# Score bank filled by ScalarE, VectorE's order in the shifted layers, and the experts' bias and gathers

## What is computed

```python
for i in range(6):
    x = attn_layer(shift_tokens(x), Wqkv[i], q_scale[i], k_scale[i], Wo[i]) + x
    x = ffn_layer(shift_tokens(x), ln_g[i], ln_b[i], W1[i], b1[i], W2[i], b2[i]) + x
# in attn_layer: q, k normed, scaled and rotated; then per window
sim = einsum('bhwie,bhwje->bhwij', q, k2) * 8
sim = where(mask, -finfo.max, sim)      # band: own window and the one before
out = softmax(sim) @ v2
# in ffn_layer: (a * gelu(gate)) @ W2 + b2, a and gate from layernorm(x) @ W1 + b1
```

```python
xin = xf[routes]                                  # 8 x 512 rows gathered
h = gelu(einsum('ekd,edf->ekf', xin, W1) + b1)
out = (einsum('ekf,efd->ekd', h, W2) + b2) * route_vals
final = zeros.at[routes].add(out)                 # rows added back
```

## Time and profile before

| | us |
|---|---|
| median of 3 runs (4852.14 to 4854.57) | 4854.38 |
| the profiled execution | 4843.04 |
| its span, first to last instruction | 4841.2 |
| shifted layers, about | 340 to 3900 |
| experts' gathers, products and additions | 4703 to 4841 |

### The profile page before, as it was taken

The page is one execution under the profiler, slowest core; times in us unless marked ns, Lnnn a source line. Parts: engine busy times, 40 slices in busy tenths (PEclk is TensorE's granted clock), DMA queues, the critical chain, the costliest instruction groups (busy, mean ns, idle before and its releaser), DMA issues. The chain is left out here.

```text
span 4841.2 us, 113325 instructions
## 1 busy us (share of the span) xinstructions
PE 4259.6 (88%) x40622; PEld 2404.1 (50%) x40622; DVE 3564.2 (74%) x8488; ACT 2826.2 (58%) x5112; POOL 2217.0 (46%) x1393
## 2 busy tenths in 40 slices
PE   8969999999999999999999999999999964746646
PEld 5645555554555555545555555555555532535534
DVE  6878888887888888878888888788888847456430
ACT  3436666666666666666666666666666635645301
POOL 0006555555555555555555555555555510030015
PEclk9989999999999999999999999999999975868558
DMA  1012222322223222232222322223222210000202
GB/s 40 1 59 65 59 58 55 78 59 56 58 53 77 64 54 59 54 77 62 54 56 60 74 63 54 58 56 74 61 60 54 58 25 1 12 1 6 77 11 30
DMA packets 187686, 245.93 MB, mean 51 GB/s; under 512 B 88661, under 2 KB 129367, under 8 KB 187224
## 3 DMA queue, kind: packets, MB, share of 16 engines
q1 hardware_dynamic: 181912, 239.95, 21.3%
q0 software_dynamic: 5632, 4.33, 0.7%
HBM read 41.13 MB, written 14.30 MB: 11 GB/s over the span
## 5 line engine op out<-in xcount | busy, mean ns | idle before, releaser
L1229 POOL TENSOR_TENSOR f_rot_a<-f_rot_a,f_norm 128x1024 f32<-128x1024 f32 x384 | 731.1, 1904 | 1106.7 <-DVE f_norm L1072 1074.2
L1221 POOL TENSOR_TENSOR f_rot_a<-f_rot_a,f_rot_b 128x1024 f32<-128x1024 f32 x384 | 907.4, 2363 | 353.8 <-issue 298.3
L830 PE MATMUL f_bank<-f_w_vo,f_xs_t 128*64 128x512 f32 x3072 | 828.5, 617 | 9.7 <-ACT f_vo L1297 9.7
L1297 ACT ACTIVATE f_vo<-f_bank 128x512 f32<-128x512 f32 x768 | 457.7, 596 | 579.0 <-PE f_bank L830 572.6
L1288 ACT ACTIVATE f_squares<-f_bank 128x512 f32<-128x512 f32 x768 | 459.1, 598 | 330.2 <-PE f_bank L817 244.5
L1051 DVE TENSOR_TENSOR f_rot_a<-f_bank,f_rot 128x512 f32<-128x512 f32 x768 | 526.8, 686 | 86.3 <-POOL f_rot_a L1221 41.6
L1054 DVE TENSOR_TENSOR f_rot_b<-f_bank,f_rot 128x512 f32<-128x512 f32 x768 | 514.2, 670 | 0.0
L1100 DVE TENSOR_REDUCE f_stat<-f_score 128x8 f32<-128x512 f32 x384 | 262.0, 682 | 280.5 <-ACT f_score L1314 280.5
L1058 DVE TENSOR_REDUCE f_sums<-f_squares 128x16 f32<-128x1024 f32 x384 | 465.1, 1211 | 3.3
L1309 ACT ACTIVATE f_k_t<-f_bank 64x512 f32<-64x512 f32 x768 | 450.4, 586 | 4.8 <-PE f_bank L852 0.3
L817 PE MATMUL f_bank<-f_w_qk,f_xs_t 128*128 128x512 f32 x768 | 431.7, 644 | 7.4 <-ACT f_xs_t L1279 5.9
(11 more groups left out here) (447 smaller groups left out, 7249.8 us busy)
## 6 DMA issues: line engine op xcount, KB each, us to landing
f_vo_off<-f_vo SPq DMA_DIRECT2D x1152, 128.0 KB, 2.3
f_vo_off<-f_vo SPq DMA_DIRECT2D x384, 64.0 KB, 2.0
f_w_qk<-in_Wqk SPq DMA_DIRECT2D x12, 512.0 KB, 5.5
f_vo_dram<-f_vo_pair SPq DMA_DIRECT2D x48, 128.0 KB, 1.8
f_x_shifted<-s_all SPq DMA_DIRECT2D x48, 128.0 KB
f_x_shifted<-s_all SPq DMA_DIRECT2D x48, 127.0 KB
f_w_vo<-f_vo_dram SPq DMA_DIRECT2D x10, 512.0 KB, 4.0
e_w<-in_e_W SPq DMA_DIRECT2D x2, 2048.0 KB
```

Source lines behind the costliest of these rows:

```text
L830: done = nc.tensor.matmul(bank[V][64 * n:64 * n + 64, :], x, w_vo[:, 4 * g:4 * g + 4, n, :], start=True, stop=True)
L1221: nc.gpsimd.tensor_tensor(rot_a[:, slot, :, :], rot_a[:, slot, :, :], rot_b[:, g, :, :], ALU.add).then_inc(rot_summed, 1)
L1229: nc.gpsimd.tensor_tensor(heads, heads, over(norm[:, 16 * g:16 * g + 16], [128, 16, HEAD_DIM]), ALU.mult).then_inc(qk_normed, 1)
L1297: nc.scalar.activation(vo[:, g, 2 * (t % 2) + j, :], flat(V), ACT.Copy).then_inc((va_copied, vb_copied)[j], 1)
```

## The change

1. **Band by ScalarE.** The matmul at L859 goes. One such matmul is done once, before the loop (`s_opened`). In its place ScalarE copies `band` (bf16, SBUF) into bank S by an activation with Copy, `seed(p, t, g)`, after the key copy of the same tile and half; `seed` takes over the wait for `shifted`, and `scores` waits for `seeded`.
2. **VectorE's order.** In step 3, `hide(p-2, 0)`, and in step 1 `store(p-3)`, come before the second part of the key rotation `rotate(p, r, 1, 1, 1)` and not after it. `hide(p-2, 1)` comes before `highest(p, r-1, 1)` and not after the query rotations and `aggregate`. The `total(p, r-1, 1)` that ended step 2 moves into step 3, behind the first key rotation; `invert(1)` follows it there.
3. **ScalarE's order.** In step 3 the `exponential(p, r-2, 1)` comes after `copy_values(r-1, 1, 0)` and `copy_q(r-1, 0)`.
4. **Experts' bias.** b2 is laid out over all 128 partitions by the host (512 KB are loaded in place of 4 KB); the four bias matmuls of each expert go; VectorE adds b2 to the whole bank in one instruction (128 x 512, PSUM to `rows`), waits for it, and then multiplies the four parts in place in SBUF.
5. **Gathers.** `BESIDE` is four: after each expert's additions four gathers follow. The memset of the ones goes.

```diff
@@ shifted_layers, TensorE
             pe.wait_ge(zeroed, 2)
+            nc.tensor.matmul(flat(S), ident_bf[:, :], band[:, 0, :], start=True, stop=True).then_inc(s_opened, 1)
...
             def scores(p, t, g):
                 pe.wait_ge(k_t_made, count(p, 2 * t + g))
-                pe.wait_ge(shifted, count(p, 2 * t + g - 1))
-                nc.tensor.matmul(flat(S), ident_bf[:, :], band[:, t % 2, :], start=True, stop=True)
+                pe.wait_ge(seeded, count(p, 2 * t + g))
@@ shifted_layers, VectorE's body
-                    if on(r - 2):
+                    if r < 3 and on(r - 2):
                         invert(1)
                     if on(r):
                         rotate(p, r, 0, 1, 1)
+                    if r == 3 and on(r - 2):
+                        total(p, r - 2, 1)
+                        invert(1)
...
                         highest(p, r - 1, 0)
-                    if on(r):
-                        rotate(p, r, 1, 1, 1)
                     if r == 1 and has(p, 3):
                         store(p - 3)
                     if r == 3 and has(p, 2):
                         hide(p - 2, 0)
+                    if on(r):
+                        rotate(p, r, 1, 1, 1)
...
                         total(p, r - 1, 0)
                         invert(0)
+                    if r == 3 and has(p, 2):
+                        hide(p - 2, 1)
+                    if on(r - 1):
                         highest(p, r - 1, 1)
...
                         aggregate()
-                    if r == 3 and has(p, 2):
-                        hide(p - 2, 1)
-                    if on(r - 1):
+                    if r != 2 and on(r - 1):
                         total(p, r - 1, 1)
@@ shifted_layers, ScalarE
+            def seed(p, t, g):
+                act.wait_ge(shifted, count(p, 2 * t + g - 1))
+                nc.scalar.activation(flat(S), band[:, t % 2, :], ACT.Copy).then_inc(seeded, 1)
...
-                    if on(r - 2):
+                    if r < 3 and on(r - 2):
                         exponential(p, r - 2, 1)
                     if on(r - 1):
                         copy_values(p, r - 1, 1, 0)
                         copy_q(p, r - 1, 0)
+                    if r == 3 and on(r - 2):
+                        exponential(p, r - 2, 1)
...
                         copy_k(p, r - 1, 0)
+                        seed(p, r - 1, 0)
                         copy_values(p, r - 1, 1, 1)
...
                         exponential(p, r - 1, 0)
                         copy_k(p, r - 1, 1)
+                        seed(p, r - 1, 1)
@@ apply_experts
-    BESIDE = 2
+    BESIDE = PARTS
...
-            nc.gpsimd.memset(ones[:, :], 1.0).then_inc(ones_set, 1)
...
-                        nc.tensor.matmul(o_bank[e % 2][:, 128 * t:128 * t + 128], h[:, e % 2, c, 128 * t:128 * t + 128], w2[:, e, c, :],
-                                         start=c == 0, stop=False)
-                    last = nc.tensor.matmul(o_bank[e % 2][:, 128 * t:128 * t + 128], ones[:, :], b2[:, DIM * e:DIM * e + DIM], start=False, stop=True)
+                        last = nc.tensor.matmul(o_bank[e % 2][:, 128 * t:128 * t + 128], h[:, e % 2, c, 128 * t:128 * t + 128], w2[:, e, c, :],
+                                         start=c == 0, stop=c == CHUNKS - 1)
...
+                nc.vector.tensor_tensor(rows[:, e % 2, :, :], o_bank[e % 2][:, :].rearrange("p (c n) -> p c n", n=DIM),
+                                        b2[:, DIM * e:DIM * e + DIM].unsqueeze(1).broadcast_to([128, PARTS, DIM]), ALU.add).then_inc(bias_added, 1)
+                dve.wait_ge(bias_added, e + 1)
                 for c in range(PARTS):
-                    last = nc.vector.tensor_scalar(rows[:, e % 2, c, :], o_bank[e % 2][:, 128 * c:128 * c + 128], taken[:, e % RING, c, DIM + e:DIM + e + 1], None, ALU.mult)
+                    last = nc.vector.tensor_scalar(rows[:, e % 2, c, :], rows[:, e % 2, c, :], taken[:, e % RING, c, DIM + e:DIM + e + 1], None, ALU.mult)
```

More of the change, by code:

```diff
@@ L569, in shifted_layers @@
         scores_done, shifted, exped, inverted = sem("scores_done"), sem("shifted"), sem("exped"), sem("inverted")
+        s_opened, seeded = sem("s_opened"), sem("seeded")
         prob_made, prob_turned, prob_t_made = sem("prob_made"), sem("prob_turned"), sem("prob_t_made")
@@ L1265, in _ @@
             act.wait_ge(zeroed, 2)
+            act.wait_ge(s_opened, 1)
             act.wait_ge(rot_out, 16)
@@ L1268, in _ @@
                 act.sem_inc(semaphore, AHEAD)
-            for semaphore in (scores_done, q_turned, k_turned, q_done, k_done, va_done, vb_done, prob_turned, mixed):
+            for semaphore in (seeded, scores_done, q_turned, k_turned, q_done, k_done, va_done, vb_done, prob_turned, mixed):
                 act.sem_inc(semaphore, AHEAD)
@@ L2729, in experts @@
         b1 = ctx.enter_context(nc.sbuf_tensor("e_b1", [128, EXPERTS * CHUNKS], F32))
-        b2 = ctx.enter_context(nc.sbuf_tensor("e_b2", [1, EXPERTS * DIM], F32))
+        b2 = ctx.enter_context(nc.sbuf_tensor("e_b2", [128, EXPERTS * DIM], F32))
         slots = ctx.enter_context(nc.sbuf_tensor("e_slots", [128, EXPERTS, CAPACITY // 128], I32))
@@ L3231, in apply_experts @@
         t_bank = ctx.enter_context(nc.psum_tensor("ea_t_bank", [128, 512], F32))
-        ones = sb("ones", [1, 128])
         taken = sb("taken", [128, RING, PARTS, ROW])
@@ L3236, in apply_experts @@
         rows = sb("rows", [128, 2, PARTS, DIM])
-        ones_set = sem("ones_set")
         gathered = [sem(f"gathered{i}") for i in range(RING)]
@@ L3240, in apply_experts @@
             sem("x_turned"), sem("x_t_made"), sem("h_done"), sem("h_made"), sem("o_done"), sem("rows_made"))
-        added = sem("added")
+        added, bias_added = sem("added"), sem("bias_added")
         ctx.callback(clear, nc, used)
@@ L3303, in second_product @@
                     for c in range(CHUNKS):
-                        nc.tensor.matmul(o_bank[e % 2][:, 128 * t:128 * t + 128], h[:, e % 2, c, 128 * t:128 * t + 128], w2[:, e, c, :],
-                                         start=c == 0, stop=False)
-                    last = nc.tensor.matmul(o_bank[e % 2][:, 128 * t:128 * t + 128], ones[:, :], b2[:, DIM * e:DIM * e + DIM], start=False, stop=True)
+                        last = nc.tensor.matmul(o_bank[e % 2][:, 128 * t:128 * t + 128], h[:, e % 2, c, 128 * t:128 * t + 128], w2[:, e, c, :],
+                                         start=c == 0, stop=c == CHUNKS - 1)
                 last.then_inc(o_done, 1)
             pe.wait_ge(w_in, 64)
-            pe.wait_ge(ones_set, 1)
             turn(0)
@@ L3342, in _ @@
         def _(dve):
+            dve.wait_ge(w_in, 64)
             for e in range(EXPERTS):
@@ L3471, in lay_out @@
     d["e_b1"] = c(f["L3_ffn_b1"].reshape(EXPERTS * CHUNKS, 128).T)
-    d["e_b2"] = c(f["L3_ffn_b2"]).reshape(1, EXPERTS * DIM)
+    d["e_b2"] = c(np.broadcast_to(f["L3_ffn_b2"].reshape(1, EXPERTS * DIM), (128, EXPERTS * DIM)))
     d["k_proj"] = c(f["L1_xattn_projection"].T)
```

## The result

The changed kernel takes 4659.59 us in the median of four runs (4656.79 to 4664.66), the kernel before 4853.26 in its four: a ratio of 0.9604, interval 0.9592 to 0.9617. It is 194 us faster; 183 were forecast. The profiled execution took 4656.79 us, where 4660 was forecast for it.

What follows compares the result with a forecast made beforehand. It took the layers as bound by TensorE's stream and its waits, the experts' end by GpSimd's queue. Layers 3.4 us x 48 = 163 plus experts 20 gave 183 us: 4660 profiled, 4671 median; own range 4635 to 4705, outer 4605 to 4755.

Steps and rivals of the forecast that it cites:

- The band: Layers: dropping eight band matmuls per pass saves TensorE 4 x 0.21 + 4 x 0.32 = 2.1 us, bounds 1.7 and 2.5.
- The seed's price: ScalarE's copy of the band into PSUM takes 0.60 us, of which 0.50 is added to its stream.
- Its slacks: Before scores, g = 0: 0.5 us in step 0, 0.05 step 1, 0.9 step 2; g = 1: 0.2 or more.
- The orders: New orders in the layers cut TensorE's waits from 3.5 to 2.2 us per pass, saving 1.3.
- the walk through step 3: Key turn's 1.31 us wait goes; scores wait 0.75 for the seed; second up projection waits 0.55, values 0.64.
- The experts: GpSimd's queue sets the end; the last addition starts at 4811.3, not 4830.8: gain 19.5 us, range 12 to 22.
- the first addition starts near 4729.3: Experts: GpSimd's first addition comes then, not at 4730.79; TensorE is 2.3 us earlier, VectorE's step 0.8 longer.
- More goes: Layers: new step 3 wait and the one for `hide(0)` don't appear; 271 + 20 us gained, 4563; chance 0.12.
- ScalarE takes TensorE's place: Each seed costs 1.0 us in ScalarE's stream, or copies shift waits; 1.4 us per pass less, 4738; chance 0.22.
- slower: Copying into a bank TensorE also uses is much dearer; at 1.7 us a seed 4896 in all; chance 0.07.
- Layers don't move: Waits go elsewhere on VectorE; only the experts give, 8 to 20 us, 4834 to 4846; chance 0.04.
- The rule against it: Experts' SBUF multiplications and GpSimd lock each other out; experts give 8 us, not 20; chance 0.4 within any case.

Runs made afterwards that it cites:

- experiment 6: Changed kernel with hide(0) in step 3 and store in step 1 moved ahead of one more rotation and highest(0): 0.9511 of the kernel before.
- experiment 4: Changed kernel with a second copy of the band, into a spare buffer, ahead of every seed: 0.9820 of the kernel before, 105 us over the change.
- experiment 5: Changed kernel with the layers' gelus replaced by Copy, so no table load before the exponential: 0.9489 of the kernel before.
- both halves: Kernel before with the experts' part alone, bias on VectorE and four gathers behind each expert's additions: 0.9959.
- gathers only: Kernel before with four gathers behind each expert's additions, bias still matmuls on TensorE: 0.9961.
- bias only: Kernel before with the experts' bias on VectorE, still two gathers behind each expert's additions: 0.9975.
- experiments 5 to 8: Changed kernel with gelus as Copy, 0.9489; separately feed-forward earlier, 0.9511, then added in turn: later probability copy, 0.9496, later third gelu, 0.9481, three gathers, 0.9473.
- band only: Kernel before with the band copied by ScalarE, orders and experts as before: 0.9864, 66 us.
- orders only: Kernel before with the new orders of VectorE and ScalarE, band still a matmul, experts as before: 0.9751, 121 us.
- every seed twice: Changed kernel with one more copy of the band, into a spare tile, before each seed: 0.9820 of the kernel before.
- experiment 3: Kernel before with the experts' part alone, 0.9959, its gathers alone, 0.9961, or its bias on VectorE alone, 0.9975.

## Why the prediction was right, point by point

- **What bounds the kernel:** right. The layers are TensorE's stream plus its waits; an edit of VectorE's order alone (experiment 6) took away two waits of 0.99 us a pass and gave 45 us.
- **The band:** right to 0.1 us, 2.18 a pass where 2.1 was taken. Taking 0.21 after a full tile and 0.32 after a narrow one was the right reading of the earlier trace rows. What it is worth alone is less, 1.42, since two waits take a third back.
- **The seed's price:** right. I took 0.60 us, and 0.50 of it in the stream. It lasts 0.583, and from the key copy before it to the next copy ScalarE takes 1.10 us where it took 0.62, so 0.49 in the stream. ScalarE's row for the seed:

```profile
L1321 ACT ACTIVATE f_bank<-f_band x384: 582/583/584, 358.0 to 3721.1; 128x512 f32<-128x512 bf16 x192
```

- **Its slacks:** partly wrong. Step 0 has 0.4 us for g = 0 and 0.06 for g = 1 (experiment 4). The sum behind them does not come out either: the terms that I listed for step 0 leave 0.2 us (2.39 less 2.2), not 0.5, and 0.3 us is likewise missing in steps 1 and 2. At 0.58 us a copy only step 3 pays for it; at 1.1 four places do. The rival of a dear seed would therefore have been dearer than I priced it: 2.07 us a pass for 0.54 more in the stream, not 1.4.
- **The orders:** the walk through step 3 held to 0.1 us at each place of the table. For the scores its own terms give 6.88 - 6.22 = 0.66 us, which is what was measured; I booked 0.75. The step that paid most, query copy ahead of the table load, was predicted at 1.31 us and is 1.30. The new wait at the scores is real, and experiment 5 ties it to the table load.
- **The experts:** the terms were right in the kernel with nothing else changed (19.2 for 19.5). In the change 5.3 us are missing; the step that failed is "the first addition starts near 4729.3", 25.2 us after the first gather; after the change that would be 4557.2, and it was 4562.4. The second product, complete at 4554.9, was in time for it; what is late is TensorE's signal that it is complete, at 4560.45, in the slow stretch.
- **The sum** is right in part by luck. Trace against trace the gain is 186 us: 172 ahead of the first gather, 14 behind it, where 163 and 20 were forecast, so an error of +9 and one of -5. Of the 172, 167 lie between the first and the last fold (47 passes by 3.55) and 5 behind the last, in a stretch of some 890 us that also differs by 4 us between kernels whose layers are the same. Within the 167 there is luck as well: a full pass gives 3.7 and not 3.4 (the walk lacked the two ends of tiles, 0.14, and had the wait at the seed 0.09 too long), but the first nine give 2.9. The 194 us between the medians are some 7 more than the traces show: the profiled execution of the kernel before is 10 us under the median of its runs, that of the change 3. No trace shows where those 7 us lie.
- **The range.** 4605 and 4755 are not halfway to the neighbours, as the prediction says; halfway to 4563 and 4738 is 4617 and 4704. The measured 4660 lies inside either, and in the narrower 4635 to 4705.
- **The rivals.** More goes: no, the two waits appeared as walked. ScalarE takes TensorE's place, and slower: no, at 583 ns. Layers don't move: no. The parts are not independent, however: 66 and 121 us alone, 172 together.
- **The rule against it** came true in a small part and cost nothing. The multiplications from SBUF beside GpSimd's additions:

```profile
L3364 DVE TENSOR_SCALAR ea_rows<-ea_rows,ea_taken x32: 279/284/595, 4561.3 to 4630.0; 128x128 f32<-128x128 f32 x32
...
L3279 POOL DMA_INDIRECT out<-ea_rows,e_slots x32: 1550/1566/1641, 4562.4 to 4644.5; - x32
```

284 ns in the median, less than the 343 ns that they took from PSUM, and additions of 1566 ns where they were 1567. But the 595 in the row is no stray: in each of the last three experts the third multiplication takes 594 or 595 ns and the fourth 465, in the change and, within 2 ns, in both halves alone. From PSUM none took over 352. They are under way in the middle of an addition on GpSimd; one such expert (the four multiplications are merged in the row, 1.06 us for the 0.88 of the first expert):

```profile
4629.28 1.55 POOL L3279 DMA_INDIRECT out<-ea_rows,e_slots  x1 [2.47 <-DMA out<-ea_rows,e_slots]
4629.37 1.06 DVE L3364 TENSOR_SCALAR ea_rows<-ea_rows,ea_taken 128x128 f32<-128x128 f32 x4
```

So VectorE is held up beside GpSimd, by up to 0.3 us a multiplication. The prediction had the size and the price wrong. It hits 6 of 32 multiplications in full, the additions don't grow, and these rows are ready a whole round of additions before GpSimd takes them, so the stage pays nothing. The Trainium skill, SBUF — State Buffer, "Who interferes with whom", describes a lock between the two engines for a whole instruction. The trace agrees in part: the long ones end 1.1 us into an addition of 1.55, and the first and second multiplication of these experts, which run in its first 0.6 us, take 280 to 291 ns. I had given the lock a chance of 0.4. I had taken the layers' median of 706 ns as the nearest row; what lengthens those runs beside the layers' GpSimd work was not tried.

## What stays open

The slow stretch in the experts. It lasts about 5 us some 20 us after the first gather, in the change, in gathers only, in bias only and in all kernels of experiments 5 to 8 (the wait before the first addition is 5.0 to 5.4 us), and it is missing in the kernel before and in band only, orders only, both halves and every seed twice (0.3 to 1.8 us). The last has the very experts' code of the change. So neither bias nor gathers nor data decide. What does is open: the program as a whole, the chip or the single execution, since each kernel was traced once and the chips split just as the stretch does (experiment 3). One more thing goes with it and is not explained. In the 60 us after the first gather the eight traces with the stretch hold 287 to 353 records of a DMA's landing, the five without 608 or 640. So a part of the stretch could also be an effect of the recording. Running the change and both halves alone on one chip, several times each, would settle the first question; it was not done.

## What to carry to other kernels

Walk the starts of one period of the bounding engine, pair by pair, and price each edit at its place: the list of waits leaves out what lies behind each instruction's modelled tail (0.16 us here), and the pairs add up to the period exactly. Add up the stages as well, and trace against trace: a total that fits can hide errors of opposite sign. Before moving work to an engine with idle time, work out its slack at each place where the bounding engine reads its result, and expect the next late producer to take part of the gain: a part that saves 2.2 us of work a pass was worth 1.42 or 1.03, by the orders around it. Put a producer that the bounding engine waits for ahead of table loads and of work whose reader is far.

## What the runs showed of the hardware

- A ScalarE copy of 128 x 512 from bf16 in SBUF into a PSUM bank that TensorE then accumulates on takes 583 ns, with a spread of 2 ns over 384 of them.
- Four multiplications of 128 x 128 fp32 from SBUF on VectorE start 0.20 us apart (0.88 us for the four) and take 284 ns each in the median. Under way in the middle of GpSimd's indirect DMA of 1.55 us they took up to 595 ns; their starts stayed 0.20 apart, and GpSimd's time did not change.
- In eight of the thirteen traces here TensorE issues instructions 0.7 to 2.4 us apart with nothing to wait for that the profile shows, and its signal for the first second product comes some 5 us late, at the same place of the experts. The code of the experts doesn't decide which.
